# State-space stage: within a state, VectorE takes each of its two sums after two scans instead of after one

## The chip, the cores and the metric

The kernel runs on one core of a Trainium2 chip. The metric is the device time of one execution in microseconds (us), taken as the median of three. Five engines work beside each other, each in the order of its own instruction list, and meet at semaphores: TensorE (PE in the profile), VectorE (DVE), ScalarE (ACT), GpSimd (POOL) and SyncE (SP), which issues the DMAs.

## What is computed

The reference is a small network: a state-space (Mamba) block, a mixture of experts, a channel mix, a linear attention and a second mixture of experts. Only the first block holds the change:

```python
dt, Bm, Cm = jnp.split(xc @ W_xproj.T, [R, R + N], axis=-1)
delta = jax.nn.softplus(dt @ W_dt.T + b_dt)
dA = jnp.exp(delta[..., None] * A)
dBx = delta[..., None] * Bm[:, :, None, :] * xc[..., None]
def step(h, t):
    dA_t, dBx_t, C_t = t
    h = dA_t * h + dBx_t
    return (h, jnp.einsum('ben,bn->be', h, C_t))
y = ys.transpose(1, 0, 2) + D_skip * xc
y = y * jax.nn.silu(z)
```

Here are 2 sequences of 2048 tokens, 512 channels (ED) and N = 16 states for each channel. Each of the 16 states of a channel is a recurrence over the tokens of its own; the output of a token is the sum over the states, each weighted by that token's C.

## The kernel before

The tokens go through the stage in eight blocks of 512, called units here; a loop of four rounds holds two units each (`hf` 0 and 1), one of each sequence. Within a unit a loop runs over the 16 states, n = 0 to 15. The 512 channels are four chunks of 128 partitions, c = 0 to 3; the 512 tokens are four tiles of 128, j = 0 to 3. For each state:

- **GpSimd** (`product`, line 400) multiplies u by the state's row of B into the buffer `hs` of the next state, n + 1, in two halves (chunks 0 and 1, then 2 and 3), and behind each half adds (`add`, line 412) one tile that ScalarE has weighted, j = 1 and then j = 3, to the sum `acc`. There are four `hs` buffers.
- **ScalarE** makes the factors dA for the next state (`factor`, line 554, one for each chunk, into PSUM), and weights the odd tiles j = 1 and j = 3 (`weighted`, line 568). `factor` of chunk c for state n + 1 waits until VectorE has scanned chunk c of state n, since both use one PSUM buffer.
- **VectorE** runs the recurrence of the four chunks in place in `hs` (`scan`, line 778) and takes the even tiles j = 0 and j = 2 into `acc` (`summed`, line 743; 740 for the first state of a sum). `summed` returns at once for j = 1 and j = 3, which are ScalarE's and GpSimd's: of the four calls in a state two do something.
- **TensorE** (`turn`, line 924) transposes the previous state's `hs`, tile by tile, into two PSUM buffers: tiles 0 and 2 into the first, 1 and 3 into the second. Tile 0 of a turn waits for all four scans of state n - 1 and for the sum of tile 2 of state n - 1; tile 2 waits for the sum of tile 0; tiles 1 and 3 wait for ScalarE in the same way.

So in state n the sums take the tiles of state n - 1, out of the turns of state n.

Around these, each engine does parts of the next unit's front end and of the last unit's back end, at fixed states. On TensorE, tables say what stands between tiles 1 and 2 (`EARLY`) and behind tile 3 (`LATE`): the gated outputs y0 to y3 at states 1 and 2 (lines 843 and 845), o0 at state 2 and o1 at state 8 (878), f0 and f1 at state 3 (855), the convolution's 16 parts at states 3 to 8 (859), dt at state 9 (867), d0 and d1 behind tile 3 of state 10 and d2 and d3 between tiles 1 and 2 of state 11 (872). ScalarE takes these out of the PSUM buffers `fx` and `fy`; at state 8 it does the silus, at state 11 the evacuation of d2 and d3 (503, 504), the exponential of the softplus (537) and only then `factor` of chunk 1 and `weighted` of tile 3. On VectorE such work stands between the two pairs of scans or behind the fourth: the statistics of x at state 1 (670), gated products at states 1 and 2 (706), residual sums (711), the root-mean-square statistics at state 10 (717, 722), the softplus parts at states 12 and 13 (684, 691, 698). GpSimd has `front_power` at state 2 (377), which waits for ScalarE.

No scheduler sets this order: it is the order of the code in each engine's block.

Of the kernel before, what the change touches and what calls it, by code (L numbers as in the profile page):

```python
# [135 lines left out]
def mamba_phase(nc, io, per):  # L136
    H, LG, R2, ident = per.H, per.LG, per.R2, per.ident
    NBUF = 4
    with ExitStack() as ctx:
# [136 lines left out]
        def turned(U, n, j):  # L276

            return lin(U, NS * TJ, TJ * n + j + 1 + TURNED)
# [384 lines left out]
        def _(dve):  # L663
# [66 lines left out]
            def summed(U, n, j, s):  # L730

                if j not in ON:
                    return
                dve.wait_ge(s_turn, turned(U, n, j))
                k = (n - 1) % NS
                weight = c_tok[s][:, j, k:k + 1]
                if k == 0:
                    if j == 0:
                        dve.wait_ge(s_free[side("ct")], count("ct", before(U)))
                    dve.tensor_scalar(acc[s][:, j, :], hT_ps[j % 2][:], weight, None, ALU.mult).then_inc(s_acc, 1)  # L740
                    return
                dve.wait_ge(s_acc, lin(U, NS * ND, ND * (n - 1) + ON.index(j) + 1 + ND))
                dve.scalar_tensor_tensor(out=acc[s][:, j, :], in0=hT_ps[j % 2][:], scalar=weight,  # L743
                                         in1=acc[s][:, j, :], op0=ALU.mult, op1=ALU.add).then_inc(s_acc, 1)
# [19 lines left out]
            with dve.Fori(0, NB) as i:  # L764
                link = Link(dve, s_d, i * PER_D + pre, pad)
                for hf in range(2):
# [3 lines left out]
                    for n in range(NS):  # L770
# [3 lines left out]
                        def scan(c):  # L774
                            if c % 2 == 0:
                                dve.wait_ge(s_dbx, lin(U, 2 * NS, 2 * n + c // 2 + 1))
                            dve.wait_ge(s_da, lin(U, NS * EC, n * EC + c + 1))
                            dve.tensor_tensor_scan(hs[k][:, c, :], dA[c][:], hs[k][:, c, :],  # L778
                                                   carry[:, hf, c, n:n + 1], ALU.mult, ALU.add).then_inc(s_scan, 1)

                        dve.wait_ge(s_carry, lin(U, NS, n + 2))
                        scan(0)
                        summed(U, n, 0, here)
                        scan(1)
                        summed(U, n, 1, here)
                        if n == 1:
                            stats(F)
# [14 lines left out]
                        if n == 15:  # L802
                            dve.wait_ge(s_full["Y"], count("r", U))
                            dve.wait_ge(s_rr, lin(U, 1, 1))
                            logits(fy, tile0).then_inc(s_free["Y"], 1)
                        scan(2)
                        summed(U, n, 2, here)
                        scan(3)
                        summed(U, n, 3, here)
                        if n == 1:  # L810
                            gated(U, 1, 1 - hf)
# [1739 lines left out]
```

## Time and profile before

| | us |
|---|---|
| median of 3 runs | 2510.96 |
| lowest and highest | 2507.06 and 2513.07 |
| the profiled execution | 2507.86 |
| its span, first to last instruction | 2506.0 |
| VectorE busy in it | 1676.5 (67%) |
| GpSimd busy in it | 1500.6 (60%) |
| TensorE busy in it | 1937.8 (77%) |

The page cuts the span into 40 slices of 62.65 us. The state-space stage takes about the first 19 of them, to some 1200 us; there GpSimd's busy tenths are 8 and 9 in nearly all slices and VectorE's 8. A row of the timeline gives the start in us from the span's beginning, the busy time, the engine, the line, the operation and its tiles, how many instructions are merged in it (x2), and, in brackets, how long the engine stood idle before it and which instruction let it go on. Busy times of neighbours on one engine overlap by a little, so the time that an instruction takes is best read from start to start.

### The profile page before, as it was taken

What the parts mean: (1) busy time and instruction counts of PE and PEld (TensorE: products, weight loads), DVE (VectorE), ACT (ScalarE), POOL (GpSimd) and SP (SyncE); (2) the same over time, 40 slices, a digit from 0 to 9 for tenths busy, and PEclk for the clock granted to TensorE, in tenths of its full rate; (3) what the DMA queues carried; (4) which work ended last, traced back from release to release, by engine and by line L of the source; (5) the groups of instructions that cost most, each with busy time, mean ns of one, the idle gap of its engine ahead of it and who ended that gap; (6) DMA issues with size and microseconds to landing.
All of it is one profiled execution on the core that took longest, in us unless ns stands there. A gap on an engine that the chain in (4) does not pass through costs nothing. (4 is left out here: it accounts for less than half of the span.)

```text
span 2506.0 us, 35735 instructions
## 1 busy us (share of the span) xinstructions
PE 1937.8 (77%) x10252; PEld 1490.7 (59%) x10253; DVE 1676.5 (67%) x3193; ACT 1196.8 (48%) x2021; POOL 1500.6 (60%) x1119
## 2 busy tenths in 40 slices
PE   6786969696878878687399999935788685699980
PEld 2445545464545455554289999933565565599970
DVE  1788888988888887886644444426743897644438
ACT  2676767767676867675132322316641442111112
POOL 1789999998989898997033333325631430255542
PEclk9887979797887878796599999977898897699995
DMA  2111111111111011110511111132100003222226
GB/s 74 34 31 47 35 48 34 43 37 37 44 30 50 32 48 35 45 37 26 210 45 48 48 46 49 48 114 81 34 9 20 9 26 126 77 71 69 69 60 196
DMA packets 77371, 139.14 MB, mean 56 GB/s; under 512 B 10449, under 2 KB 48465, under 8 KB 76450
## 3 DMA queue, kind: packets, MB, share of 16 engines
q1 hardware_dynamic: 63586, 100.19, 12.2%
q0 software_dynamic: 13632, 37.24, 4.8%
q8 instruction: 55, 0.90, 0.1%
q14 instruction: 98, 0.80, 0.1%
HBM read 105.38 MB, written 32.01 MB: 55 GB/s over the span
## 5 line engine op out<-in xcount | busy, mean ns | idle before, releaser
L778 DVE TENSOR_TENSOR_SCAN a_hs<-a_dA,a_carry,a_hs 128x512 f32<-128x512 f32 x512 | 637.4, 1269 | 27.3 <-POOL a_hs L400 23.0
L400 POOL TENSOR_TENSOR a_hs<-a_u,a_b_bc 128x1024 f32<-128x1024 f32 x258 | 624.3, 2422 | 0.4
L924 PE MATMUL a_h_ps<-k_ident,a_hs 128*128 128x128 f32 x2064 | 338.8, 317 | 182.5 <-DVE a_hs L778 112.4
L924 PEld LDWEIGHTS a_h_ps<-k_ident,a_hs 128*128 128x128 f32 x2064 | 282.4, 164 | 301.6 <-DVE a_hs L778 135.3
L554 ACT ACTIVATE a_dA<-a_delta,a_a_neg 128x512 f32<-128x512 f32 x512 | 351.7, 688 | 106.1 <-DVE a_hs L778 103.6
L412 POOL TENSOR_TENSOR a_acc<-a_acc,a_part 128x512 f32<-128x512 f32 x242 | 323.3, 1336 | 73.8 <-ACT a_part L568 72.6
L743 DVE SCALAR_TENSOR_TENSOR a_acc<-a_h_ps,a_c_tok,a_acc 128x512 f32<-128x512 f32 x242 | 177.5, 734 | 112.5 <-PE a_h_ps L924 112.3
L568 ACT ACTIVATE a_part<-a_h_ps,a_c_tok 128x512 f32<-128x512 f32 x242 | 165.6, 684 | 153.0 <-PE a_h_ps L924 138.7
L1224 POOL DMA_INDIRECT expert_rows<-m0e_ys,k_pair x71 | 74.1, 1044 | 236.4 <-DVE m0e_ys L1280 225.2
L1290 DVE TENSOR_TENSOR m0e_hT<-m0e_gs,m0e_u 128x512 f32<-128x512 f32 x70 | 48.1, 687 | 186.7 <-ACT m0e_gs L1243 186.7
L1243 ACT ACTIVATE m0e_gs<-m0e_g 128x512 f32<-128x512 f32 x71 | 42.4, 597 | 269.7 <-PE m0e_u L1321 269.7
L1247 ACT ACTIVATE m1e_hT<-m1e_u 128x512 f32<-128x512 f32 x71 | 42.4, 597 | 226.4 <-PE m1e_u L1321 226.4
L859 PE MATMUL a_fx<-a_hT,a_w_x 128*128 128x512 f32 x288 | 139.8, 622 | 7.9 <-ACT a_halo L490 7.9
L1321 PE MATMUL m1e_u<-m1e_xT,m1e_wu 128*128 128x128 f32 x1136 | 140.2, 277 | 0.1
L1321 PE MATMUL m0e_g<-m0e_xT,m0e_wg 128*128 128x128 f32 x1136 | 140.1, 277 | 0.0
L1321 PE MATMUL m0e_u<-m0e_xT,m0e_wu 128*128 128x128 f32 x1136 | 139.5, 276 | 0.0
L1270 DVE TENSOR_SCALAR m1e_xT<-m1e_x,k_ln_w,k_ln_b 128x128 f32<-128x128 f32 x142 | 51.8, 406 | 131.0 <-PE m1e_x L1309 130.9
L1331 PE MATMUL m0e_y<-m0w_down,m0e_hT 128*128 x568 | 134.5, 380 | 0.2 <-DVE m0e_ys L1280 0.2
L1321 PEld LDWEIGHTS m1e_u<-m1e_xT,m1e_wu 128*128 128x128 f32 x1136 | 134.1, 194 | 0.5 <-issue 0.5
L1321 PEld LDWEIGHTS m0e_g<-m0e_xT,m0e_wg 128*128 128x128 f32 x1136 | 134.2, 194 | 0.1
L1331 PE MATMUL m1e_y<-m1w_down,m1e_hT 128*128 x568 | 134.2, 379 | 0.0
L1224 POOL DMA_INDIRECT expert_rows<-m1e_ys,k_pair x71 | 70.0, 986 | 106.3 <-DVE m1e_ys L1280 91.8
(429 smaller groups left out, 3879.7 us busy)
## 6 DMA issues: line engine op xcount, KB each, us to landing
a_b_bc<-b_rows SPq DMA_DIRECT2D x132, 256.0 KB, 3.1
c_y<-expert_rows SPq DMA_DIRECT2D x16, 512.0 KB, 5.6
q_y<-expert_rows SPq DMA_DIRECT2D x16, 512.0 KB, 5.7
a_xl<-in_L_attn_x SPq DMA_DIRECT2D x9, 512.0 KB, 3.6
norm_rows<-a_shared SPq DMA_DIRECT2D x9, 512.0 KB, 2.9
m0w_up<-in_m_up SPq DMA_DIRECT2D x1, 4096.0 KB, 12.3
m0w_gate<-in_m_gate SPq DMA_DIRECT2D x1, 4096.0 KB, 22.1
m0w_down<-in_m_down SPq DMA_DIRECT2D x1, 4096.0 KB, 32.4
```

The source lines that it names most:

```text
L400: pool.tensor_tensor(hs[n % NBUF][:, half, :], u[s][:, half, :], b_bc[:, n % NBUF:n % NBUF + 1, :].broadcast_to([P, 2, T]), ALU.mult).then ...
L412: pool.tensor_tensor(acc[s][:, j, :], acc[s][:, j, :], part[:, j // 2, :], ALU.add).then_inc(s_add, 1)
L554: act.activation(dA[c][:], delta[s][:, c, :], ACT.Exp, scale=a_neg[:, c, k:k + 1]).then_inc(s_da, 1)
L568: act.activation(to, hT_ps[j % 2][:], ACT.Copy, scale=c_tok[s][:, j, k:k + 1]).then_inc(s_part, 1)
L743: dve.scalar_tensor_tensor(out=acc[s][:, j, :], in0=hT_ps[j % 2][:], scalar=weight, in1=acc[s][:, j, :], op0=ALU.mult, op1=ALU.add).then_i ...
L778: dve.tensor_tensor_scan(hs[k][:, c, :], dA[c][:], hs[k][:, c, :], carry[:, hf, c, n:n + 1], ALU.mult, ALU.add).then_inc(s_scan, 1)
L859: last = pe.matmul(ps[:], w_x[:, q, d, k * P:(k + 1) * P], hT[:, d, q:q + T], start=q == 0 and d == 0, stop=q == KC - 1 and d == DC - 1)
L924: last = pe.transpose(hT_ps[j % 2][:, c * P:(c + 1) * P], hs[(n - 1) % NBUF][:, c, j * P:(j + 1) * P], ident[:])
L1224: pool.indirect_dma_start(io["expert_rows"], bass.IndirectOffsetOnAxis(ap=per.pair[:, s:s + 1], axis=0), ys[s % 2][:], None).then_inc(s_st ...
L1270: last = dve.tensor_scalar(xT[k][:, c, :], x_ps[:, c, :], scale[:, c:c + 1], shift[:, c:c + 1], ALU.mult, ALU.add)
L1321: last = pe.matmul(ps[k][:, f, :], w[k][:, c, f * P:(f + 1) * P], xT[k][:, c, :], start=c == 0, stop=c == DC - 1)
L1331: last = pe.matmul(y_ps[k][:], hT[k][:, c, :], w_down[:, c, bass.ds(e * D, D)], start=c == 0, stop=c == FC - 1)
```

## The change

In each state the first sum moves from behind scan 0 to behind scan 1, and the second from behind scan 2 to behind scan 3. Nothing is added or removed, and the other work at the middle and the end of a state keeps its place behind both.

```diff
                         scan(0)
+                        scan(1)
                         summed(U, n, 0, here)
-                        scan(1)
                         summed(U, n, 1, here)
...
                         scan(2)
+                        scan(3)
                         summed(U, n, 2, here)
-                        scan(3)
                         summed(U, n, 3, here)
```

VectorE's list at state 10 (`a_hs2` is that state's buffer, `a_dA0` and `a_dA1` the factors of chunks 0 and 1, `a_acc0` the sum, `a_h_ps0` the transposed tile, `a_pad` and `a_st2` the start of the root-mean-square statistics), before:

```order
L776 REGISTER_ALU [waits a_carry]
L778 SCALAR_TENSOR_TENSOR a_hs2<-a_dA0,a_carry,a_hs2 128x512 [waits a_dA,a_dBx]
L734 REGISTER_ALU
L743 SCALAR_TENSOR_TENSOR a_acc0<-a_h_ps0,a_c_tok0,a_acc0 128x512 [waits a_summed_by_dve,a_h_transposed]
L777 REGISTER_ALU
L778 SCALAR_TENSOR_TENSOR a_hs2<-a_dA1,a_carry,a_hs2 128x512 [waits a_dA]
L67 MEMSET a_pad 128x1 [waits a_x_task_free]
L717 BN_STATS a_st2<-k_hidden 128x6
```

The same place on VectorE after:

```order
L776 REGISTER_ALU [waits a_carry]
L778 SCALAR_TENSOR_TENSOR a_hs2<-a_dA0,a_carry,a_hs2 128x512 [waits a_dA,a_dBx]
L777 REGISTER_ALU
L778 SCALAR_TENSOR_TENSOR a_hs2<-a_dA1,a_carry,a_hs2 128x512 [waits a_dA]
L734 REGISTER_ALU
L743 SCALAR_TENSOR_TENSOR a_acc0<-a_h_ps0,a_c_tok0,a_acc0 128x512 [waits a_summed_by_dve,a_h_transposed]
L67 MEMSET a_pad 128x1 [waits a_x_task_free]
L717 BN_STATS a_st2<-k_hidden 128x6
```

The scan of chunk 1 no longer stands behind the sum's wait for the transposed tile.

VectorE's list at state 3 (`a_hs3`), where both sums can be seen, before:

```order
L778 SCALAR_TENSOR_TENSOR a_hs3<-a_dA0,a_carry,a_hs3 128x512 [waits a_dA,a_dBx]
L734 REGISTER_ALU
L743 SCALAR_TENSOR_TENSOR a_acc0<-a_h_ps0,a_c_tok0,a_acc0 128x512 [waits a_summed_by_dve,a_h_transposed]
L777 REGISTER_ALU
L778 SCALAR_TENSOR_TENSOR a_hs3<-a_dA1,a_carry,a_hs3 128x512 [waits a_dA]
L776 REGISTER_ALU
L778 SCALAR_TENSOR_TENSOR a_hs3<-a_dA2,a_carry,a_hs3 128x512 [waits a_dA,a_dBx]
L734 REGISTER_ALU
L743 SCALAR_TENSOR_TENSOR a_acc0<-a_h_ps0,a_c_tok0,a_acc0 128x512 [waits a_summed_by_dve,a_h_transposed]
L777 REGISTER_ALU
L778 SCALAR_TENSOR_TENSOR a_hs3<-a_dA3,a_carry,a_hs3 128x512 [waits a_dA]
```

And after:

```order
L778 SCALAR_TENSOR_TENSOR a_hs3<-a_dA0,a_carry,a_hs3 128x512 [waits a_dA,a_dBx]
L777 REGISTER_ALU
L778 SCALAR_TENSOR_TENSOR a_hs3<-a_dA1,a_carry,a_hs3 128x512 [waits a_dA]
L734 REGISTER_ALU
L743 SCALAR_TENSOR_TENSOR a_acc0<-a_h_ps0,a_c_tok0,a_acc0 128x512 [waits a_summed_by_dve,a_h_transposed]
L776 REGISTER_ALU
L778 SCALAR_TENSOR_TENSOR a_hs3<-a_dA2,a_carry,a_hs3 128x512 [waits a_dA,a_dBx]
L777 REGISTER_ALU
L778 SCALAR_TENSOR_TENSOR a_hs3<-a_dA3,a_carry,a_hs3 128x512 [waits a_dA]
L734 REGISTER_ALU
L743 SCALAR_TENSOR_TENSOR a_acc0<-a_h_ps0,a_c_tok0,a_acc0 128x512 [waits a_summed_by_dve,a_h_transposed]
```

Each sum stands one scan later, and scans 1 and 3 stand one sum earlier. The lists of the other engines are the same in both kernels.

## Rows read from the trace of the kernel before

**Rows 1.** The page: busy time of each engine over the whole span.

```profile
PE 1937.8 (77%) x10252; PEld 1490.7 (59%) x10253; DVE 1676.5 (67%) x3193; ACT 1196.8 (48%) x2021; POOL 1500.6 (60%) x1119
```

**Rows 2.** Who waited for whom, 100 to 1150 us: us in total, times, longest.

```profile
DVE a_acc L743 <- PE a_h_ps L924: 106.9, 72, 3.6
...
POOL a_acc L412 <- ACT a_part L568: 72.6, 39, 3.6
...
POOL a_pw L377 <- ACT a_pv L460: 15.0, 7, 2.4
```

**Rows 3.** Busy time of each engine in a stretch of one unit's length.

```profile
502.00:639.00 137.00, 107.92 (x461) 70.97 (x462) 116.41 (x128) 96.47 (x166) 124.99 (x71) 0.84 0.13 40
```

**Rows 4.** Timeline of VectorE, states 9 to 11 of the fourth unit.

```profile
569.06 2.45 DVE L778 TENSOR_TENSOR_SCAN a_hs<-a_dA,a_carry,a_hs 128x512 f32<-128x512 f32 x2
573.39 0.75 DVE L743 SCALAR_TENSOR_TENSOR a_acc<-a_h_ps,a_c_tok,a_acc 128x512 f32<-128x512 f32 x1 [1.88 <-PE a_h_ps L924]
574.06 1.27 DVE L778 TENSOR_TENSOR_SCAN a_hs<-a_dA,a_carry,a_hs 128x512 f32<-128x512 f32 x1
575.26 0.42 DVE L717 BATCH_NORM_STATS2 a_st<-k_hidden 128x6 f32 x1
...
576.99 1.25 DVE L778 TENSOR_TENSOR_SCAN a_hs<-a_dA,a_carry,a_hs 128x512 f32<-128x512 f32 x1
...
578.80 2.45 DVE L778 TENSOR_TENSOR_SCAN a_hs<-a_dA,a_carry,a_hs 128x512 f32<-128x512 f32 x2
```

**Rows 5.** Timeline of TensorE, states 10 and 11 of the same unit.

```profile
576.79 1.02 PE L872 MATMUL a_fy<-a_dbc,a_w_dt 64*128 64x512 f32 x2
580.13 1.44 PE L924 MATMUL a_h_ps<-k_ident,a_hs 128*128 128x128 f32 x8 [2.32 <-DVE a_hs L778]
...
583.37 1.91 PE L872 MATMUL a_fy<-a_dbc,a_w_dt 64*128 64x512 f32 x2
```

**Rows 6.** Timeline of ScalarE, the same states.

```profile
578.27 0.69 ACT L554 ACTIVATE a_dA<-a_delta,a_a_neg 128x512 f32<-128x512 f32 x1 [1.31 <-DVE a_hs L778]
...
588.89 0.68 ACT L568 ACTIVATE a_part<-a_h_ps,a_c_tok 128x512 f32<-128x512 f32 x1
```

**Rows 7.** Timeline of GpSimd, the same states.

```profile
584.33 2.36 POOL L400 TENSOR_TENSOR a_hs<-a_u,a_b_bc 128x1024 f32<-128x1024 f32 x1
589.73 1.27 POOL L412 TENSOR_TENSOR a_acc<-a_acc,a_part 128x512 f32<-128x512 f32 x1 [3.04 <-ACT a_part L568]
```

**Rows 8.** Timeline of VectorE, TensorE and GpSimd, states 3 and 4 of that unit.

```profile
520.00 0.72 DVE L743 SCALAR_TENSOR_TENSOR a_acc<-a_h_ps,a_c_tok,a_acc 128x512 f32<-128x512 f32 x1
...
520.77 1.09 PE L924 MATMUL a_h_ps<-k_ident,a_hs 128*128 128x128 f32 x8 [0.98 <-DVE a_acc L743]
522.68 5.39 PE L859 MATMUL a_fx<-a_hT,a_w_x 128*128 128x512 f32 x8 [0.81 <-ACT a_halo L490]
...
529.90 1.27 POOL L412 TENSOR_TENSOR a_acc<-a_acc,a_part 128x512 f32<-128x512 f32 x1 [2.37 <-ACT a_part L568]
```

**Rows 9.** Timeline of VectorE, state 5: one of the convolution's states.

```profile
535.45 0.75 DVE L743 SCALAR_TENSOR_TENSOR a_acc<-a_h_ps,a_c_tok,a_acc 128x512 f32<-128x512 f32 x1 [0.78 <-PE a_h_ps L924]
```

**Rows 10.** Timeline of GpSimd: `front_power` at state 2 of units four to seven.

```profile
508.76 1.65 POOL L377 TENSOR_TENSOR a_pw<-a_pv,a_halfneg 128x8 f32<-128x8 f32 x1 [2.25 <-ACT a_pv L460]
...
645.55 1.65 POOL L377 TENSOR_TENSOR a_pw<-a_pv,a_halfneg 128x8 f32<-128x8 f32 x1 [2.25 <-ACT a_pv L460]
...
782.21 1.65 POOL L377 TENSOR_TENSOR a_pw<-a_pv,a_halfneg 128x8 f32<-128x8 f32 x1 [1.95 <-ACT a_pv L460]
...
918.85 1.65 POOL L377 TENSOR_TENSOR a_pw<-a_pv,a_halfneg 128x8 f32<-128x8 f32 x1 [2.02 <-ACT a_pv L460]
```

**Rows 11.** Timeline of TensorE, sixth unit, state 3: the convolution's first two parts.

```profile
796.12 3.70 PE L859 MATMUL a_fx<-a_hT,a_w_x 128*128 128x512 f32 x8 [0.81 <-ACT a_halo L490]
```

**Rows 12.** Timelines of VectorE (state 15) and TensorE (y0, state 1), behind GpSimd.

```profile
619.83 1.28 DVE L778 TENSOR_TENSOR_SCAN a_hs<-a_dA,a_carry,a_hs 128x512 f32<-128x512 f32 x1 [1.24 <-POOL a_hs L400]
...
638.74 2.07 PE L843 MATMUL a_fy<-a_xc,a_diag_d 128*128 128x512 f32 x2 [2.68 <-POOL a_acc L412]
```

## The prediction

> **What bounds the kernel now.** Start with the page: over the whole span no engine is busy more than 77% [rows 1], so the stage has to be looked at by itself. One stretch as long as a unit has GpSimd busy 125.0 of 137 us, VectorE 116.4, TensorE 107.9 and ScalarE 96.5 [rows 3]. GpSimd's work in a unit is therefore the floor, and what lies above it, some 12 us, is GpSimd standing idle. The list of waits says for whom: for ScalarE's weighted tile 72.6 us in 39 waits, and 15.0 us in 7 waits for the moments at state 2 [rows 2]. With eight units to the stage that is some 9 and 2 us in each. A unit takes 136.8 us, read from one `front_power` to the next [rows 10].
>
> The larger number in that list is VectorE's: 106.9 us in 72 waits for a transposed tile, ahead of a sum [rows 2]. This is what the change touches, and it would be a mistake to count it as a gain. VectorE has some 20 us of idle time in each unit [rows 3]; filling a wait there only helps if something that GpSimd waits for comes earlier. So each wait has to be followed to GpSimd.
>
> **What the change does to one state.** VectorE's work is the same: four scans, two sums. From start to start a scan takes 1.20 us (574.06 to 575.26) and a sum 0.67 (573.39 to 574.06) [rows 4]. The last of the six still ends at the same time if nothing waits, and tile 0 of the next turn needs all of them, so it moves nowhere. Two things do move. (a) Where the first sum waits for tile 0, scan 1 is done inside that wait, and all that follows on VectorE comes up to 1.20 us earlier. (b) Where tile 0 is on time, the first sum ends 1.20 us later, and tile 2 of the turn, which waits for it, starts up to 1.20 us later; behind it in TensorE's list stand tile 3 and the `LATE` work, and behind tile 3 ScalarE's weighted tile and GpSimd's second add. The second sum's place costs nothing: only tile 0 of the next state waits for it, and that waits for scan 3 too. SyncE's loads wait for GpSimd's products and are not passed.
>
> **Part 1: states 4 to 8, the convolution.** Each first sum waits about 0.8 us [rows 9], since TensorE runs without a gap there. Scan 1 fits into that wait and VectorE then waits again at the next sum: TensorE sets the pace and keeps it, tile 2 has a convolution part ahead of it as cover. 0 us.
>
> **Part 2: state 10.** The order on VectorE is two scans, a wait of 1.88, the first sum at 573.39, scan 1 at 574.06, the statistics, scan 2 at 576.99, the second sum, scan 3 and the next state's scan 0 from 578.80 [rows 4]. TensorE stands idle 2.32 us until scan 3 is done, and starts the turn of state 11 at 580.13 [rows 5]. ScalarE too waits 1.31 us, for scan 2 [rows 6]. Behind the turn come d2 and d3, the latter from 583.37 for 1.91 [rows 5], then on ScalarE their evacuation, the exponential and the weighted tile at 588.89 [rows 6]; and only that releases GpSimd at 589.73, after 3.04 us of idle time [rows 7]. This is the place where VectorE is on the path. With the change scan 1 runs inside the 1.88 us, which is longer than 1.20: 1.88 - 1.20 leaves 0.68 of the wait. Scan 2, scan 3, the turn of state 11, d2, d3 and the weighted tile come 1.20 us earlier, ScalarE's wait of 1.31 covers its share of it, and GpSimd's stall shrinks from 3.04 to 1.84. Gain 1.20 us for a unit. What is late next is the same chain, with less idle time ahead of it. From there to the next unit's state 1 GpSimd has no wait to speak of, VectorE waits for it (1.24 us at state 15), and y0 on TensorE as well (2.68 us) [rows 12], so the gain is carried over into the next unit.
>
> **Part 3: state 3.** Here tile 0 is on time: the first sum stands at 520.00, TensorE waits 0.98 us for it, starts tiles 2 and 3 at 520.77, then waits 0.81 us for ScalarE's halo and begins the convolution at 522.68 [rows 8]. With the sum 1.20 later the two tiles start at 521.97 and, at 1.09 us, end at 523.06. Of the 1.20 the wait of 0.81 hides its part, so the convolution starts 0.39 us later at most; busy times of neighbours overlap by some tenths, so it may be nothing, and I take the middle, 0.2. The convolution is on the path (GpSimd then waits 2.37 us for the turn of state 4, [rows 8]), and the delay goes through the states 4 to 9 to state 10. Loss 0.2 us for a unit, bounds 0 and 0.39.
>
> **Part 4: states 12 to 1.** Case (b) applies: ScalarE's weighted tile 3 may come up to 1.20 us later. But there GpSimd runs ahead and the others wait for it, at state 15 by 1.24 us [rows 12], more than the delay. 0 us; above it I keep the 0.39 of state 3, the nearest case of a late tile 2, as a bound.
>
> **The sum.** 1.20 - 0.20 = 1.00 us for a unit, eight units: 8.0 us. The profiled execution took 2507.86, so 2499.9 by it; it lies 3.1 below the median, and the same 8.0 from the median of 2510.96 gives **2503 us**. The bounds of parts 2 to 4 put the gain between 8 x (1.20 - 0.39 - 0.39) = 3.4 and 8 x 1.20 = 9.6, so 2501 to 2508, and the scatter of runs adds 2 to 3 us to either side.
>
> **The clock, which the rivals hang on.** TensorE's clock is granted at 1.2 or 2.4 GHz, and the rows show both: d1 took 1.02 for two matmuls, d3, the same form, 1.91 just after the idle 2.32 us [rows 5]; the convolution's first two parts took 5.39 us in the fourth unit and 3.70 in the sixth, though both had a gap of 0.81 before them [rows 8, 11]. The change takes 1.2 us from the gap at state 10, and at state 3 it joins two gaps of 0.98 and 0.81 into one of about 2.2. The Trainium skill (TensorE: Matmul & The Clock Gate, section "HAM oscillation — how this bites in real kernels") says that idle gaps between bursts of matmuls make the clock fall back and that each burst after one starts slow; by it the first would be for the change and the second against it. The rows agree that slow matmuls stand behind gaps, but 0.81 came out both ways.
>
> **Rival 1: the clock stays high through state 11.** For it: the idle 2.32 becomes 1.1. Against it: 0.98 and 0.81 were enough in the fourth unit. Then d2 and d3 take 1.02 and not 1.91 each, 1.8 us less on the path to GpSimd's stall. GpSimd is ready at 584.33 + 2.36 = 586.69 [rows 7], so no more than 3.04 can be won there; ScalarE's evacuations then become the limit, and I take the middle between 1.0 and 3.0: 2.0 us for a unit, 16 in all, **2495 us**.
>
> **Rival 2: no change.** The gap at state 3 brings the slow clock into the units that don't have it. The price is 5.39 - 3.70 = 1.69 us; in the five of eight units whose convolution starts fast (the sixth stands for them, [rows 11]; the other three are as in [rows 8]) that is 8.5 us, and 8.0 - 8.5 is zero: **2511 us**. Against it: the unit with the slow start took 645.55 - 508.76 = 136.79 us and the one with the fast start 918.85 - 782.21 = 136.64 [rows 10], so the 1.69 us is given back within the unit, nearly whole.
>
> **Rival 3: slower.** The one long gap of 2.2 us at state 3 is as long as that of state 10, behind which d2 and d3 both ran slow. If the clock then stays low for both pairs of the convolution's first parts in every unit, a unit pays up to 2 x 1.69 = 3.38, of which three units pay 1.69 already: 8 x 3.38 - 3 x 1.69 - 8.0 = 14 us, **2525 us**. It decides from 1.0 us on, the gain of a unit. For it: all of this is on the path to GpSimd. Against it: the same give-back as in rival 2, and the transposes run in the middle of the gap's old place.
>
> **How the numbers follow.** The forecast 0.45; rival 1 0.15; rival 2 0.23; rival 3 0.17. What a measurement of this kernel can tell from no change is about 0.2%, 5 us: faster means below 2506. Of the forecast 0.43 and all of rival 1 lie there: faster 0.58. Rival 2 and the rest of the forecast: same 0.25. Rival 3: slower 0.17. The range of the forecast alone, scatter included, is 2499 to 2510. For 8 in 10 it has to reach down to rival 1 and up past no change: 2493 to 2515, which leaves out rival 3 and a little of rival 1.
>
> **What the profile after would show.** Right: GpSimd's stall at state 11 near 1.8 us in place of 3.0; TensorE's idle time ahead of the turn of state 11 near 1.1 in place of 2.3; VectorE's wait at state 10's first sum near 0.7; TensorE's wait ahead of tile 2 in state 3 near 2.2; from `front_power` to `front_power` 135.8 us. Total waits of VectorE ahead of the sums fall by far more (some 0.8 in each convolution state) than the time does. Wrong: a convolution that starts slow in all units, and a stall above 2.4 at state 4 (rivals 2 and 3); d2 and d3 at 1.0 each (rival 1); or a stall of GpSimd between states 12 and 1, where none is now, which would say that tile 2's delay reaches it and part 4 was mis-sized.

## The result, and the profile after

| | before | after |
|---|---|---|
| median of 5 runs (us) | 2507.86 | 2484.55 |
| lowest and highest | 2503.31 and 2513.07 | 2481.17 and 2489.07 |
| the profiled execution | 2507.86 | 2481.17 |
| its span | 2506.0 | 2479.5 |
| a unit, `front_power` to `front_power` | 136.5 to 137.4 | 133.1 to 133.2 |
| GpSimd's four stalls in the fourth unit, state 2 / 4 / 9 / 11 | 2.25 / 2.37 / 3.53 / 3.04 | 2.63 / 0.72 / 3.53 / 0.76 |

After to before is 0.9905, 95% interval 0.9885 to 0.9925: faster by 0.95%, 23 us by the medians. I had forecast 8 us, 2503, and a range that ended at 2493. The time lies below it.

The state-space stage ends where GpSimd issues the first gather of the next one. That row stands in the timeline of GpSimd, of before:

```profile
1252.78 1.18 POOL L1216 DMA_INDIRECT m0e_xs<-norm_rows,k_token  x1 [41.81 <-SPq L1161]
```

and of after:

```profile
1223.22 1.18 POOL L1216 DMA_INDIRECT m0e_xs<-norm_rows,k_token  x1 [41.81 <-SPq L1161]
```

So the stage became 29.6 us shorter, 3.7 us for each of eight units. Behind it the first execution took 1253.2 us and the second 1256.2; over all the profiled executions of this case that rest lies between 1248.8 and 1259.6, whatever was changed in the stage. The place of this row is therefore a cleaner measure of a change than the total, though it comes from one execution for each kernel.

The page after, to be read beside [rows 1]:

```profile
PE 1906.0 (77%) x10252; PEld 1475.5 (60%) x10253; DVE 1680.2 (68%) x3193; ACT 1186.9 (48%) x2021; POOL 1499.7 (60%) x1119
```

VectorE and GpSimd are busy as long as before. TensorE, with the same 10252 instructions, is busy 31.8 us less. An order on VectorE gives TensorE no other work, so the same matmuls ran faster; the windows further down show that it was the clock.

The list of waits after, 100 to 1150 us (us in total, times, longest), beside [rows 2]:

```profile
DVE a_acc L743 <- PE a_h_ps L924: 53.0, 50, 2.5
POOL a_acc L412 <- ACT a_part L568: 40.3, 25, 3.5
POOL a_pw L377 <- ACT a_pv L460: 18.4, 7, 2.6
```

VectorE's wait for tiles is halved, from 106.9 to 53.0. GpSimd's wait for weighted tiles fell from 72.6 to 40.3; this is the gain. GpSimd's wait at state 2 for ScalarE's `a_pv`, called the moments here, took 3.4 us back (15.0 to 18.4).

Timeline of GpSimd after, fourth unit, its four stalls and the start of the next unit:

```profile
497.59 1.65 POOL L377 TENSOR_TENSOR a_pw<-a_pv,a_halfneg 128x8 f32<-128x8 f32 x1 [2.63 <-ACT a_pv L460]
516.92 1.28 POOL L412 TENSOR_TENSOR a_acc<-a_acc,a_part 128x512 f32<-128x512 f32 x1 [0.72 <-ACT a_part L568]
555.95 1.27 POOL L412 TENSOR_TENSOR a_acc<-a_acc,a_part 128x512 f32<-128x512 f32 x1 [3.53 <-ACT a_part L568]
574.49 1.27 POOL L412 TENSOR_TENSOR a_acc<-a_acc,a_part 128x512 f32<-128x512 f32 x1 [0.76 <-ACT a_part L568]
630.65 1.65 POOL L377 TENSOR_TENSOR a_pw<-a_pv,a_halfneg 128x8 f32<-128x8 f32 x1 [2.62 <-ACT a_pv L460]
```

The unit takes 630.65 - 497.59 = 133.06 us in place of 136.79 [rows 10]. Its stalls fell by 3.55 us (11.19 to 7.64), which is nearly all of the 3.73. The stall at state 11 went from 3.04 to 0.76 and not to 1.84; the one at state 4 from 2.37 to 0.72, where I expected a small loss. All eight units are alike now in this execution.

VectorE after, state 10, beside [rows 4]:

```profile
560.41 0.75 DVE L743 SCALAR_TENSOR_TENSOR a_acc<-a_h_ps,a_c_tok,a_acc 128x512 f32<-128x512 f32 x1 [0.90 <-PE a_h_ps L924]
```

and TensorE after, states 10 and 11, beside [rows 5]:

```profile
563.82 1.02 PE L872 MATMUL a_fy<-a_dbc,a_w_dt 64*128 64x512 f32 x2
566.02 1.09 PE L924 MATMUL a_h_ps<-k_ident,a_hs 128*128 128x128 f32 x8 [1.19 <-DVE a_acc L743]
567.04 1.12 PE L872 MATMUL a_fx<-a_dbc,a_w_dt 64*128 64x512 f32 x2
568.00 1.02 PE L872 MATMUL a_fy<-a_dbc,a_w_dt 64*128 64x512 f32 x2
```

The wait of 1.88 became 0.90, TensorE's idle time ahead of the turn of state 11 became 1.19 in place of 2.32, near the 0.7 and 1.1 of the forecast. But d2 and d3 take 1.12 and 1.02 where they took 2.07 and 1.91. The granted clock of such stretches stands in a view by windows (start:end, length, busy time of PE, PEld, DVE, ACT and POOL with the number of instructions, then the granted clock, where 1.00 is 2.4 GHz and 0.50 is 1.2 GHz, then the DMA's busy share and its GB/s). Of before, the convolution's start and the turn of state 11 with d2 and d3:

```profile
522.00:528.00 6.00, 5.32 (x9) 2.32 (x10) 4.09 (x4) 2.96 (x7) 5.27 (x3) 0.72 0.12 44
...
580.00:586.00 6.00, 5.87 (x16) 3.00 (x17) 4.26 (x5) 5.14 (x11) 6.00 (x4) 0.56 0.14 46
```

and of after the same two:

```profile
511.00:517.00 6.00, 6.00 (x25) 3.40 (x24) 6.00 (x7) 3.55 (x7) 5.21 (x4) 1.00 0.13 46
...
566.00:572.00 6.00, 5.18 (x26) 3.11 (x27) 6.00 (x7) 6.00 (x11) 6.00 (x5) 1.00 0.13 48
```

In before each unit has two low stretches in the part of it that GpSimd waits for: d2 and d3 in all eight, and besides either the convolution's first parts (5.4 in place of 3.7 us, three units) or dt (4.56 to 4.68 in place of 3.60 in four units, 5.29 in the first). This is dt in the fifth unit of before:

```profile
704.85 4.68 PE L867 MATMUL a_fy<-a_xc,a_w_proj 128*96 128x512 f32 x8
```

After has none of them. So the question for the experiments was how much of the 29.6 us is the clock's and how much the order's, and what in the order moves the clock.

### The profile page after: what moved, and what is told of

The parts are those of the page before. It is cut to its first block and busy times, and to the rows that moved or that the text cites. A ratio compares the mean times of both kernels' runs of the same rounds, so it can differ in the third digit from the quotient of the medians.

```text
span 2479.5 us, 35735 instructions
## 1 busy us (share of the span) xinstructions
PE 1906.0 (77%) x10252; PEld 1475.5 (60%) x10253; DVE 1680.2 (68%) x3193; ACT 1186.9 (48%) x2021; POOL 1499.7 (60%) x1119
## 5 line engine op out<-in xcount | busy, mean ns | idle before, releaser
L778 DVE TENSOR_TENSOR_SCAN a_hs<-a_dA,a_carry,a_hs 128x512 f32<-128x512 f32 x512 | 628.7, 1267 | 41.9 <-POOL a_hs L400 24.9
L924 PE MATMUL a_h_ps<-k_ident,a_hs 128*128 128x128 f32 x2064 | 333.2, 313 | 185.2 <-DVE a_acc L743 160.1
L924 PEld LDWEIGHTS a_h_ps<-k_ident,a_hs 128*128 128x128 f32 x2064 | 279.8, 162 | 301.0 <-DVE a_acc L743 124.8
L412 POOL TENSOR_TENSOR a_acc<-a_acc,a_part 128x512 f32<-128x512 f32 x242 | 322.5, 1333 | 41.9 <-ACT a_part L568 40.3
L1321 PE MATMUL m0e_u<-m0e_xT,m0e_wu 128*128 128x128 f32 x1136 | 139.2, 276 | 0.0
L859 PE MATMUL a_fx<-a_hT,a_w_x 128*128 128x512 f32 x288 | 134.6, 602 | 1.4 <-ACT a_halo L490 1.4
L1331 PE MATMUL m0e_y<-m0w_down,m0e_hT 128*128 x568 | 134.5, 380 | 0.2 <-DVE m0e_ys L1280 0.2
L1321 PEld LDWEIGHTS m0e_g<-m0e_xT,m0e_wg 128*128 128x128 f32 x1136 | 134.2, 194 | 0.1
L1331 PE MATMUL m1e_y<-m1w_down,m1e_hT 128*128 x568 | 134.2, 379 | 0.0
```

The source lines that it names most:

```text
L412: pool.tensor_tensor(acc[s][:, j, :], acc[s][:, j, :], part[:, j // 2, :], ALU.add).then_inc(s_add, 1)
L859: last = pe.matmul(ps[:], w_x[:, q, d, k * P:(k + 1) * P], hT[:, d, q:q + T], start=q == 0 and d == 0, stop=q == KC - 1 and d == DC - 1)
L924: last = pe.transpose(hT_ps[j % 2][:, c * P:(c + 1) * P], hs[(n - 1) % NBUF][:, c, j * P:(j + 1) * P], ident[:])
L1321: last = pe.matmul(ps[k][:, f, :], w[k][:, c, f * P:(f + 1) * P], xT[k][:, c, :], start=c == 0, stop=c == DC - 1)
L1331: last = pe.matmul(y_ps[k][:], hT[k][:, c, :], w_down[:, c, bass.ds(e * D, D)], start=c == 0, stop=c == FC - 1)
```

## Experiments

Conv, dt and d2 stand for the convolution's first eight matmuls, the eight of dt and the two of d2; they run low or high as the granted clock is 1.2 or 2.4 GHz. The units are those of the profiled execution, one for each kernel, and the eighth unit's length can't be read. Line numbers behind an added line are higher by as much: the turn is L924, L927, L941 or L942, and a row with `a_w_out` and 128x128 is an added transpose. Where transposes are added, their results are never used: they read a weight and write a PSUM buffer that is free at that point and is overwritten next. Ratios are to before, run beside them on the same chip.

### Which sum it is

The order of before, with only the first sum moved:

```diff
                         scan(0)
-                        summed(U, n, 0, here)
                         scan(1)
+                        summed(U, n, 0, here)
```

> Only the first sum of each state stands behind scan 1; the second stands behind scan 2 as before. Theory 1 (what counts is that scan 1 runs inside the wait ahead of the first sum, and that TensorE's clock then stays high through d2 and d3): the whole gain, some 23 us. Theory 2 (the second sum's place matters too, since scan 3 ends a sum's length, 0.65 us, earlier and ScalarE's last factor with it): clearly less, 10 to 18 us.

Measured: 2479.41 us, ratio 0.9886 (0.9866 to 0.9906). Units 133.1 to 133.3 but for the first (135.1), and GpSimd's stall at state 11, fourth unit:

```profile
577.24 1.27 POOL L412 TENSOR_TENSOR a_acc<-a_acc,a_part 128x512 f32<-128x512 f32 x1 [0.75 <-ACT a_part L568]
```

Only the second sum moved (the same edit behind `scan(2)`):

> Only the second sum stands one scan later. Theory 1: no change, within 3 us, and d2 and d3 still at the low clock (2.07 and 1.91 us). Theory 2: 5 us or more of the gain.

Measured: 2506.85 us, ratio 1.0000 (0.9989 to 1.0011). TensorE, states 10 and 11:

```profile
580.66 1.33 PE L924 MATMUL a_h_ps<-k_ident,a_hs 128*128 128x128 f32 x8 [2.37 <-DVE a_acc L743]
...
583.80 1.91 PE L872 MATMUL a_fy<-a_dbc,a_w_dt 64*128 64x512 f32 x2
```

The whole gain is the first sum's; of the second sum's place nothing can be measured, as the prediction said.

### Which state it is

The first sum moved in state 10 alone:

```diff
                         scan(0)
+                        if n == 10:
+                            scan(1)
                         summed(U, n, 0, here)
-                        scan(1)
+                        if not (n == 10):
+                            scan(1)
```

> The first sum stands behind scan 1 in state 10 alone, all else as before. Theory 1a (state 10 is the one place): GpSimd's stall at state 11 goes from 3.0 to under 1 us, d2 and d3 take 1.12 and 1.02 us, and 16 us or more of the gain of 23 are there; the slow stretch that each unit had at the convolution's start or at dt stays or not, and that is worth the rest, 8 x 1.0 us. Theory 1b (several states share it, the clock at the convolution and dt among them through the order at state 3): 8 to 10 us, the 1.2 us of the order at state 10 alone.

Measured: 2495.90 us, ratio 0.9953 (0.9935 to 0.9971), 12 us, between the two expectations. The units are of two kinds: 1, 2, 3 and 5 have dt, d2 and d3 high and take 133.3 to 133.5 us (but for the first, 135.0, whose conv is low), as in after, and the other four have them low and take 136.5 where it can be read, as in before. TensorE in a unit of the first kind, the fifth:

```profile
695.66 3.60 PE L870 MATMUL a_fy<-a_xc,a_w_proj 128*96 128x512 f32 x8
...
705.27 1.09 PE L927 MATMUL a_h_ps<-k_ident,a_hs 128*128 128x128 f32 x8 [1.12 <-DVE a_hs L778]
...
707.26 1.02 PE L875 MATMUL a_fy<-a_dbc,a_w_dt 64*128 64x512 f32 x2
```

and in one of the second, the sixth:

```profile
828.33 0.66 PE L927 MATMUL a_h_ps<-k_ident,a_hs 128*128 128x128 f32 x4 [2.58 <-ACT a_part L568]
828.83 5.29 PE L870 MATMUL a_fy<-a_xc,a_w_proj 128*96 128x512 f32 x8
...
840.14 1.97 PE L927 MATMUL a_h_ps<-k_ident,a_hs 128*128 128x128 f32 x8 [1.12 <-DVE a_hs L778]
...
843.91 1.91 PE L875 MATMUL a_fy<-a_dbc,a_w_dt 64*128 64x512 f32 x2
```

The granted clock of the two turns with d2 and d3 (the third and the last row of one answer):

```profile
705.00:711.00 6.00, 4.86 (x25) 3.04 (x26) 6.00 (x7) 6.00 (x12) 6.00 (x5) 1.00 0.13 46
...
840.00:846.00 6.00, 5.86 (x13) 2.98 (x14) 4.38 (x5) 4.71 (x10) 6.00 (x4) 0.50 0.14 46
```

This is one program, twice the same instructions with the same idle 1.12 us ahead of the turn, once at 2.4 and once at 1.2 GHz. In this execution the low turns are those of the four units whose dt ran low, 11 us earlier. What differs between the two kinds is the clock, and it is worth 136.5 - 133.4 = 3.1 us. The order at state 10 did its part in the low kind too: the first unit of before has the same three times (3.70, 5.29 and 2.07) and takes 137.4 us, 0.9 more, with one more stall of GpSimd, 1.20 us just ahead of that of state 11, which the sixth unit here doesn't have.

The reverse: the change everywhere but in the first sum of state 10. The diff is against before and shows the first sum; the second stands as in the change, here and in the next kernel.

```diff
                         scan(0)
+                        if n != 10:
+                            scan(1)
                         summed(U, n, 0, here)
-                        scan(1)
+                        if not (n != 10):
+                            scan(1)
```

> Both sums as in the changed kernel in all states, but in state 10 the first sum stands ahead of scan 1 as before. Theory 1a: no gain to speak of, within 3 us of the kernel before; GpSimd's stall at state 11 near 3.2 us. Theory 1b: 10 us or more of gain, with the convolution's first parts and dt at the high clock in all units.

Measured: 2516.03 us, ratio 1.0040 (1.0026 to 1.0055): slower than before by 8 us. Seven units start their convolution low (4.7 to 5.3 us), three of them have a low dt (5.29) as well, and d2 and d3 are low in all; these units take 136.9 us, or 139.2 where dt is low too, and the first, with a high conv, 135.0. TensorE in state 3 of the fourth unit:

```profile
522.89 1.27 PE L927 MATMUL a_h_ps<-k_ident,a_hs 128*128 128x128 f32 x8 [2.16 <-DVE a_acc L743]
523.95 5.16 PE L862 MATMUL a_fx<-a_hT,a_w_x 128*128 128x512 f32 x8
```

Here is the one joined gap of 2.16 us at state 3 with a low clock behind it, which rivals 2 and 3 of the prediction were about. That the joining did it isn't shown: the first unit of this kernel has the same gap with a high clock behind it, and so have all eight of the changed kernel. So the first sum of state 10 is needed for the gain, but it isn't enough for all of it.

State 3 apart: the change, with the first sum of state 3 where it was.

```diff
                         scan(0)
+                        if n != 3:
+                            scan(1)
                         summed(U, n, 0, here)
-                        scan(1)
+                        if n == 3:
+                            scan(1)
```

> The changed kernel with the first sum of state 3 ahead of scan 1, as before. By the prediction's part 3 the new order costs 0.2 us a unit there, so this is 1.6 us faster than the changed kernel, by the traces so far 0.1 a unit, not to be told from zero. If the joined gap at state 3 matters to the clock, for or against, it shows as slow starts of the convolution or of dt in some units: 1.7 or 1.0 us for each such unit.

Measured: 2483.78 us, ratio 0.9903 (0.9885 to 0.9922), the same as the change itself. The gap is split again, and GpSimd's stall at state 4 is 0.65 in place of 0.72:

```profile
510.78 1.09 PE L927 MATMUL a_h_ps<-k_ident,a_hs 128*128 128x128 f32 x8 [0.99 <-DVE a_acc L743]
512.69 3.70 PE L862 MATMUL a_fx<-a_hT,a_w_x 128*128 128x512 f32 x8 [0.81 <-ACT a_halo L490]
```

```profile
518.22 1.28 POOL L412 TENSOR_TENSOR a_acc<-a_acc,a_part 128x512 f32<-128x512 f32 x1 [0.65 <-ACT a_part L568]
```

The sum's later place at state 3 costs 0.07 us in a unit, and the joined gap does no harm in the changed kernel. Its first unit has a low conv (5.40) behind the split gap.

### The clock held up by hand

To take the clock out of the comparison, transposes fill TensorE's gaps. First a small fill: the order of before, four transposes ahead of the turn of state 11.

```diff
+                if j == 0 and n == 11:
+                    for c in range(EC):
+                        pe.transpose(hT_ps[0][:, c * P:(c + 1) * P], w_out[:, c, 0:P], ident[:])
```

> The kernel before, with four transposes more on TensorE (into the PSUM buffer that the turn overwrites) inside its idle time ahead of the turn of state 11, behind the second sum of state 10 and ahead of the wait for scan 3; the order on VectorE is the old one. Theory C (most of the gain is TensorE's clock, which the shorter gap keeps up): d2 and d3 take 1.12 and 1.02 us, GpSimd's stall at state 11 falls by about 1.8 us, and the time by 10 to 15 us. Theory O (the gain is the order on the path and its followers; the clock is a by-product): within 3 us of before.

Measured: 2505.01 us, ratio 0.9990 (0.9976 to 1.0004). TensorE in the fourth unit:

```profile
575.94 0.66 PE L923 MATMUL a_h_ps<-k_ident,a_w_out 128*128 128x128 f32 x4 [1.13 <-DVE a_acc L743]
577.13 1.61 PE L927 MATMUL a_h_ps<-k_ident,a_hs 128*128 128x128 f32 x8 [0.54 <-DVE a_hs L778]
...
580.54 1.91 PE L872 MATMUL a_fy<-a_dbc,a_w_dt 64*128 64x512 f32 x2
```

No gap there is longer than 1.13 us now, and d2 and d3 still run low, in all eight units. Yet conv is high in all eight, where before had it low in three, and dt is low in seven. Either the clock has nothing to do with gaps here, or the fill was too small or in the wrong place: it stands behind VectorE's sum, in the middle of the gap. The next kernels decide against the first, though not between the other two, as their fill is larger and also stands at the gap's start: the order of before with 8 transposes ahead of tile 2 of state 3, 16 ahead of tile 3 of state 9 and 16 ahead of the turn of state 11.

```diff
+            FILL = {(3, 2): 2, (9, 3): 4, (11, 0): 4}
+
+            def filler(ps, k):
+                for _ in range(k):
+                    for c in range(EC):
+                        pe.transpose(ps[:, c * P:(c + 1) * P], w_out[:, c, 0:P], ident[:])
```

> The kernel before, with transposes into free PSUM in three of TensorE's gaps: 8 ahead of tile 2 of state 3, 16 ahead of tile 3 of state 9, 16 ahead of the turn of state 11. They take 0.88 and 1.76 us at the high clock. Theory C: conv, dt, d2 and d3 all at the high clock, 15 to 24 us faster than before. Theory O: within 3 us.

Measured: 2488.29 us, ratio 0.9918 (0.9896 to 0.9940), with 40 useless transposes added to each unit and the order untouched. TensorE, then GpSimd, fourth unit:

```profile
566.57 1.97 PE L919 MATMUL a_h_ps<-k_ident,a_w_out 128*128 128x128 f32 x16
568.94 1.09 PE L941 MATMUL a_h_ps<-k_ident,a_hs 128*128 128x128 f32 x8 [0.41 <-DVE a_hs L778]
...
570.93 1.02 PE L872 MATMUL a_fy<-a_dbc,a_w_dt 64*128 64x512 f32 x2
```

```profile
577.49 1.27 POOL L412 TENSOR_TENSOR a_acc<-a_acc,a_part 128x512 f32<-128x512 f32 x1 [1.94 <-ACT a_part L568]
```

All eight units have convolution, dt, d2 and d3 at 2.4 GHz. Useless work has no other way to save time that the traces show, so against before this is the clock's share: 2507.94 - 2488.29 = 19.7 us. What is left at state 11 is a stall of 1.94 to 1.99, and this is the order's.

The same with the changed order (16, 16 and 8 transposes):

> The changed kernel with the same gaps filled (16, 16 and 8 transposes). With the clock high in both, the difference to the filled kernel before is the order's own share. Theory C: 8 us, the 1.0 us for a unit that the prediction worked out, and this kernel equals the changed one within 4 us. Theory O: it stays 20 us or more ahead of the filled kernel before.

Measured: 2478.75 us, lowest 2476.4 and highest 2479.03, ratio 0.9882 (0.9863 to 0.9902). The stall at state 11:

```profile
573.30 1.27 POOL L412 TENSOR_TENSOR a_acc<-a_acc,a_part 128x512 f32<-128x512 f32 x1 [0.74 <-ACT a_part L568]
```

With the clock high on both sides, the order takes the stall from 1.94 to 0.74 in the fourth unit, the 1.20 us of one scan (1.20 to 1.25 over the eight), and the time from 2488.29 to 2478.75: **9.5 us**. By the end of the stage it is 1230.9 - 1221.9 = 9.0. The fills at states 3 and 11 differ in size between the two, so the comparison isn't of the order alone. Part 2 of the prediction was right; it sits on top of the clock's share.

The two shares make 29.2 us, as the stage of the profiled execution says (29.6), but the medians of before and after differ by 23. The changed kernel's five executions go from 2481.17 us at a mean granted clock of 0.866 to 2489.07 at 0.859, the longer ones at the lower clocks. So some of them probably had low stretches that the profiled one, the shortest, has not; which, no trace shows.

### Where the low clock comes from

Three more kernels, run in one batch, take the fills of the order of before apart.

```diff
-            FILL = {(3, 2): 2, (9, 3): 4, (11, 0): 4}
+            FILL = {(11, 0): 4}
```

> The order of before, with 16 transposes (results unused) in TensorE's list ahead of the turn of state 11 and nowhere else. Local theory: the gap in front of a piece of work decides that piece's clock. Then d2 and d3 take 1.12 and 1.02 us in all units, GpSimd's stall at state 11 is 1.9 to 2.0 us, and the convolution's first parts (5.4) or dt (4.6 to 5.3) are still slow in each unit: 8 x 1.7 = 13 us gained, about 2495. History theory: the slow stretches move together, so that which of convolution and dt is slow changes too, or both become fast: 20 us gained, about 2488, as with the three fills. Rival, that the fill at state 11 is not what did it: d2 and d3 stay at 2.07 and 1.91, 2508.

> The order of before, with 16 transposes (results unused) in the gap ahead of tile 3 of state 9, in front of dt, and nowhere else. Local theory: dt takes 3.60 us in all units, convolution slow in about three and d2, d3 slow (2.07, 1.91) in all eight: at most five units gain 1 us, 2503 to 2508. History theory: with dt fast everywhere the convolution becomes slow or fast in all units, or d2 and d3 become fast in some: 2490 to 2500, or 2510.

 (`FILL = {(9, 3): 4}`)

> The order of before, with 8 transposes (results unused) in the gap ahead of tile 2 of state 3 and 16 ahead of tile 3 of state 9, none at state 11. Local theory: convolution 3.70 and dt 3.60 in all units, d2 and d3 2.07 and 1.91 in all; a unit 135.8 us (134.1 of the kernel with all three fills + 1.66 of the longer stall at state 11), 7 us gained, about 2501, and together with the kernel that fills state 11 alone the 20 us of all three. History theory: d2 and d3 are fast in some or all units too, 2488 to 2495.

 (`FILL = {(3, 2): 2, (9, 3): 4}`)

Measured, with the place of the first gather (the stage's end) and the units of the profiled execution:

| fill (order of before) | median | ratio (95%) | stage ends | conv | dt | d2 | stall at 11 | unit |
|---|---|---|---|---|---|---|---|---|
| none (before) | 2507.86 | | 1252.8 | 5.4 in 3, 3.7 in 5 | 3.6 in 3, 4.6 or so in 4, 5.29 in 1 | 2.07 | 2.8 to 3.6 | 136.5 to 137.4 |
| 9 | 2506.28 | 0.9994 (0.9985, 1.0004) | 1244.1 | 3.70 | 3.60 | 2.07 | 3.0 to 3.6 | 135.3 to 136.0 |
| 3 and 9 | 2500.80 | 0.9971 (0.9960, 0.9983) | 1244.3 | 3.70 | 3.60 | 2.07 | 3.0 to 3.6 | 135.3 to 136.1 |
| 11 | 2499.93 | 0.9969 (0.9955, 0.9983) | 1241.4 | 3.70 | 5.29 in 5 | 1.12 | 2.42, or 1.94 | 136.0, or 134.2 |
| 3, 9 and 11 | 2488.29 | 0.9918 (0.9896, 0.9940) | 1230.9 | 3.70 | 3.60 | 1.12 | 1.94 to 1.99 | 133.9 to 134.5 |

TensorE with the fill at state 11 alone, third unit, dt and then d3:

```profile
427.57 5.29 PE L867 MATMUL a_fy<-a_xc,a_w_proj 128*96 128x512 f32 x8
...
442.06 1.02 PE L872 MATMUL a_fy<-a_dbc,a_w_dt 64*128 64x512 f32 x2
```

and with the fills at 3 and 9, fourth unit:

```profile
518.49 3.70 PE L859 MATMUL a_fx<-a_hT,a_w_x 128*128 128x512 f32 x8 [0.81 <-ACT a_halo L490]
...
574.26 1.97 PE L941 MATMUL a_h_ps<-k_ident,a_hs 128*128 128x128 f32 x8 [2.32 <-DVE a_hs L778]
...
578.03 1.91 PE L872 MATMUL a_fy<-a_dbc,a_w_dt 64*128 64x512 f32 x2
```

Two things follow. At state 11 a gap of 2.3 us does decide: filled, d2 and d3 are high in all eight units, also where dt was low just before; unfilled (2.32 to 2.38 us), they are low in all units of the five kernels that have it so, 40 of 40. The local theory's 2501 for the fills at 3 and 9 came out at 2500.8, perhaps by luck, since the fill at 9 alone has the same clocks in its profile and gained 0.6 us in place of 6.1. But for the convolution the local theory falls: the fill at state 11 makes it high in all units though its own gaps are untouched, and so does the fill at state 9; and with the fill at state 11 dt is low for its whole length in five units (5.29 us), where before had that in one and 4.6 in four. These fills stand 80 to 90 us ahead of the next convolution. The gain with the fill at 11, 7.0 us, is neither theory's (13 and 20). Against before in the same batch, 2506.92, the medians of the two partial kernels add up to 7.0 + 6.1 = 13 us and not to 20, while the stage ends of the profiled executions do add up (11.4 + 8.5 = 19.9 beside 21.9). Executions of one kernel differ in this: the profiled one of the fill at state 11 took 2492.04 us and its six others 2497.81 to 2502.60, and the fill at state 9 alone has its stage 8.7 us shorter in the profile and almost nothing in the median of ten runs. Which of its other executions ran low where, no profile here shows.

### The rest of the unit

GpSimd's stall of 2.62 us for the moments, at state 2, is behind a stretch with a low clock too (0.60 on average from 480 to 500 us of after). The changed order, with 8 transposes ahead of tile 0 or tile 2 at six places of the states 14 to 1 and 12 ahead of y0, none at the states 3, 9 and 11:

```diff
+            FILL = {(14, 2): 2, (15, 0): 2, (15, 2): 2, (0, 0): 2, (0, 2): 2, (1, 0): 2}
...
+                        filler(fy, 3)
                         pe.wait_ge(s_acc, lin(U, NS * ND, 2 * ND))
```

> The changed kernel with transposes in TensorE's gaps of states 14, 15, 0 and 1 (8 ahead of tiles 0 and 2, 12 ahead of y0), where its clock is low. If the clock is up when y0 starts, y0 takes 1.9 in place of 3.6 us and GpSimd's stall at the moments goes from 2.62 us to near 0.9: 10 to 14 us faster than the changed kernel. If the fill doesn't raise it, or delays the turns, no gain or up to 10 us lost.

Measured: 2479.55 us, ratio 0.9882 (0.9861 to 0.9903). The mean granted clock rose from 0.866 to 0.895, and the time can't be told from the changed kernel's (0.9885 to 0.9925), where 10 to 14 us were expected. GpSimd in the fourth unit:

```profile
496.02 1.65 POOL L377 TENSOR_TENSOR a_pw<-a_pv,a_halfneg 128x8 f32<-128x8 f32 x1 [0.48 <-ACT a_pv L460]
...
517.26 1.28 POOL L412 TENSOR_TENSOR a_acc<-a_acc,a_part 128x512 f32<-128x512 f32 x1 [2.44 <-ACT a_part L568]
```

The moments' stall fell from 2.63 to 0.48, and the next one rose from 0.72 to 2.44, since the convolution now starts low, in six of the eight units. TensorE at state 3, of this kernel:

```profile
509.20 1.09 PE L942 MATMUL a_h_ps<-k_ident,a_hs 128*128 128x128 f32 x8 [2.16 <-DVE a_acc L743]
510.13 5.29 PE L859 MATMUL a_fx<-a_hT,a_w_x 128*128 128x512 f32 x8
```

and of after:

```profile
510.56 1.09 PE L924 MATMUL a_h_ps<-k_ident,a_hs 128*128 128x128 f32 x8 [2.16 <-DVE a_acc L743]
511.49 3.60 PE L859 MATMUL a_fx<-a_hT,a_w_x 128*128 128x512 f32 x8
```

The same gap of 2.16 us, and the low clock behind it in one kernel and not in the other. The fills ahead of it are all that differs, so what lies before the gap counts too: 2.1 us won, 1.7 given back at state 4. The seventh unit of this kernel shows the same at state 11. Its dt ran low, as in the low units of the kernel changed at state 10 alone, but d2 and d3 behind an idle 1.19 us ran high:

```profile
954.05 5.29 PE L867 MATMUL a_fy<-a_xc,a_w_proj 128*96 128x512 f32 x8
...
965.43 1.09 PE L942 MATMUL a_h_ps<-k_ident,a_hs 128*128 128x128 f32 x8 [1.19 <-DVE a_acc L743]
...
967.41 1.02 PE L872 MATMUL a_fy<-a_dbc,a_w_dt 64*128 64x512 f32 x2
```

So a low dt doesn't settle the clock of state 11 either.

All fills together, with the changed order:

> The changed kernel with both sets of transposes, those of the filled kernel (states 3, 9, 11) and the late ones (states 14 to 1 and ahead of y0). Theory C2 (the late fill's gain of 2.0 us a unit at the moments was lost to the slow start of the convolution, behind the gap at state 3): with that gap filled the convolution's first parts take 3.6 us, GpSimd's stall at state 4 is 0.7, and a unit takes 131.0 to 131.5 in place of 133.1 us: 12 to 17 us faster than the changed kernel. Theory F (something else gives the gain back, the POOL queue or the filler's own time): as the changed kernel, within 4 us.

and with the order of before:

> The same two sets of transposes with the sums in the old order. The order's own share is the difference to the kernel above: 8 to 10 us if it doesn't hang on the clock, as between the two filled kernels; if both fill and order only shift where the gaps fall, it can be anything.

Measured: 2476.82 us (2472.18 to 2484.08), ratio 0.9871 (0.9844 to 0.9898), and 2484.68 us (2478.67 to 2488.70), ratio 0.9907 (0.9890 to 0.9925). The order is worth 7.9 us between them by the medians; the profiled executions, of which the second is the shortest of its four, end the stage at the same 1223, so this pair doesn't settle it. The 12 us or more expected of the first did not come: the moments' stall varies between 0.58 and 2.04 from unit to unit. The fills may delay turns themselves, since they wait for ScalarE to free their buffer; this is argued from the code and not shown. The cause of the variation is not settled, and I would not call this kernel faster than the changed one.

## Why the prediction was wrong

**What bounds the kernel, and how to follow a wait to GpSimd**: right. The fourth unit's gain is the sum of GpSimd's stalls, within 0.2 us. VectorE's wait isn't the measure: in the kernel changed everywhere but in state 10 it fell from 106.9 to 89.4 us in the same stretch, while GpSimd's rose from 72.6 to 79.4 and the time by 8.

**Part 2, state 10**: the term was right, 1.20 us a unit. It measured 1.20 in the fourth unit's stall and 9.5 us in the time with the clock held high. I named the gap at state 11, and that it would shrink to 1.1 (1.19).

**Part 3, state 3**: the sign was right and the size too large, 0.07 us in place of 0.2. **Part 1** was right: 0, TensorE keeps the pace. But I also wrote that VectorE's waits would fall by 0.8 us in each convolution state, against part 1 itself: they are 0.78 in both kernels. The fall by half comes from state 4 (2.45 to 0.57 in the fourth unit), state 10 (1.88 to 0.90) and state 12 (2.11 and 0.49 to none), where the tile now comes in time or nearly so. **Part 4** was right as far as GpSimd goes: no stall appeared between states 12 and 1.

**The sum**, 1.00 us a unit, would by these be 1.20 - 0.07 = 1.13, 9.0 us. That is the order's share, and it was not where the error lay.

**The step that failed is the one on the clock.** The forecast took for granted that TensorE's work keeps the clock that it had, and I gave a change of it as a rival with 0.15. The runs show d2 and d3 at 1.12 and 1.02 us in place of 2.07 and 1.91, and a clock's share of 19.7 us. My argument against it was that gaps of 0.98 and 0.81 were enough to lower the clock in the fourth unit [rows 8]. The same rows gave the answer against that: the same gaps came out high in the sixth [rows 11], so they proved nothing either way, while at state 11 the 2.3 us gap had a low clock behind it in eight units of eight. Beside an always there stood a sometimes, and the change removed half of the always. That should have made rival 1 the likeliest or an equal.

Its price was too small as well. I had 2.0 us a unit where convolution and dt stay as they are, 16 us in all. The change freed them too (1.69 and 1.0 us or more in their rows), and with all three high a unit loses 2.5 us more than by the order: 19.7 us. I had capped the gain at GpSimd's own 3.04 at state 11, forgetting that the low convolution also stands in the stall of state 4 [rows 8]. Rival 2 said that 1.69 us of a slow convolution is given back within the unit, nearly whole, since the two kinds of unit are equally long [rows 10]. That was a wrong reading: the units are equally long because those with a fast convolution had a slow dt instead. With both fast a unit takes 135.7 on average, a whole microsecond less (the fills at 3 and 9). An equality of two totals isn't evidence that a term is free, until the other terms have been compared too.

**Rivals 2 and 3** did not come true. Their sign, a convolution that starts low behind the joined gap, appears in seven units where state 10 is left out (8 us slower), but that the joined gap is its cause isn't shown. In the changed kernel it is harmless. The Trainium skill (TensorE: Matmul & The Clock Gate, section "HAM oscillation — how this bites in real kernels") says that bursts after idle gaps start slow; state 11 agrees, 2.3 us in front of 2.07 and 1.91. Its "no PE-idle gaps" rule is stated for gaps longer than any of these, and the low clock behind 2.3 us, in all eight units, says that here shorter gaps can do it too.

**What remains open.** Why the changed order keeps convolution and dt high, and why d2 and d3 are high behind an idle 1.1 to 1.2 us in all units of some kernels and in half of them in another. The gap in front of dt is the same 2.57 or 2.58 us in all: high in after and in half the units of the kernel changed at state 10 alone, low in the other half. The first sums of states other than 10 are part of it, since with state 10 alone four units of eight stay low, and state 3 by itself isn't the one that matters. Which of the other states it is was not tried.

## What to carry to other kernels

When a change touches the idle time in front of matmuls, count for each such gap how often the work behind it ran low and how often high, over all repetitions; a gap with a low clock behind it every time is a term of the sum and not a rival. Taking half of it away can bring that work back to 2.4 GHz: in eight units of eight with the whole change, in four of eight with state 10 alone. Compare all the parts of two equally long repetitions before calling one of them free. To split a measured gain, fill the gaps with useless transposes in both orders, and look in the profile whether the clock is high in both: the difference that is left is then the order's own.

## What the runs showed of the hardware

- The clock was worth more than the order's own share of 9.5 us: 19.7 us of 2508 by forty useless transposes of 128x128 in each unit, with the same instructions otherwise.
- A fill of 4 transposes (0.66 us) between idle times of 1.13 and 0.54 us did not keep the clock up; 16 in one piece (1.97 us), at the start of the gap, did, in every unit of the three kernels that had them at state 11.
- The same gap can have either clock behind it: 2.16 us at state 3 gave 3.60 us in one kernel and 5.29 in another; 1.12 us at state 11 gave 1.02 and 1.91 for d3 in two units of one execution.
- A higher mean clock isn't a shorter time: 0.866 and 0.895 with the same stage end, 1223.2 and 1223.6 us.
- A fill can move the low stretch elsewhere: with 16 at state 11 the convolution, 80 us later, was high in eight units in place of five, and dt low for all its 5.29 us in five in place of one.
